# Head-narrow cross attentions tiled in row and column quarters, a wide one in row halves, and other unread products

## What is computed

```python
def _L0_xattn_ref(x, context, mask, g_norm, null_kv, Wq, Wkv, Wout, g_out):
    HEADS, DIM_HEAD = (16, 64)
    ...
    k = jnp.concatenate([nk, k], axis=2)
    v = jnp.concatenate([nv, v], axis=2)
    ...
    sim = jnp.einsum('bhid,bhjd->bhij', q, k)
    ...
    attn = jax.nn.softmax(sim.astype(jnp.float32), axis=-1).astype(sim.dtype)
    out = jnp.einsum('bhij,bhjd->bhid', attn, v)
    ...
def _L2_xattn_ref(query, key_value, Wq, bq, Wk, bk, Wv, bv, Wo, bo):
    ...
    attn = jnp.einsum('bhqd,bhkd->bhqk', q, k) * scale
    attn = jnp.clip(attn, -CLAMP, CLAMP)
    attn = jax.nn.softmax(attn, axis=-1)
    ...
    x = jnp.einsum('bhqk,bhkd->bqhd', attn, v).reshape(B, Nq, Cq)
    return x @ Wo + bo
```

## Time and profile before

| | |
|---|---|
| time, median of 3 runs | 1818.76 us (1816.85 to 1821.48) |
| the profiled execution: its time | 1830.47 us |
| its span | 1828.6 us |
| its mean granted clock of PE | 0.907 |
| PE busy (products) | 1582.6 us, 87% |
| PE weight loads (PEld), beside them | 953.6 us, 52% |
| DVE busy | 1039.3 us, 57% |
| ACT busy | 678.5 us, 37% |
| POOL busy | 376.1 us, 21% |

### The profile page before, as it was taken

One profiled execution on the slowest core, in us unless ns is written; L12 is line 12 of the kernel. 1 busy time (PEld: TensorE's weight loads), 2 busy tenths in 40 slices (PEclk: granted clock), 3 DMA queues, 4 the chain that ended last, 5 costly groups with the idle time before them and its releaser, 6 DMA issues. The chain is left out here.

```text
span 1828.6 us, 24507 instructions
## 1 busy us (share of the span) xinstructions
PE 1582.6 (87%) x9019; PEld 953.6 (52%) x9027; DVE 1039.3 (57%) x1963; ACT 678.5 (37%) x1652; POOL 376.1 (21%) x366
## 2 busy tenths in 40 slices
PE   6999899999999989968988848836989988899996
PEld 3665446445555565554567535522435555564444
DVE  4676574334554555567392366489875554465665
ACT  3774331333555534423102134213555555460001
POOL 3000120001000000033011034255764433410000
PEclk8999999998787889989687979977999999899999
DMA  3000002210000000000104000000111100100000
GB/s 128 2 2 4 1 1 102 97 46 13 1 1 1 1 14 8 9 3 0 60 1 156 9 29 39 20 15 24 35 35 18 18 13 14 17 7 24 23 23 12
DMA packets 14075, 46.92 MB, mean 26 GB/s; under 512 B 3032, under 2 KB 4870, under 8 KB 13328
## 3 DMA queue, kind: packets, MB, share of 16 engines
q1 hardware_dynamic: 13968, 45.49, 8.1%
HBM read 40.73 MB, written 0.56 MB: 23 GB/s over the span
## 5 line engine op out<-in xcount | busy, mean ns | idle before, releaser
L503 DVE TENSOR_REDUCE quad_max<-psum 128x1 f32<-128x128 f32 (+3 forms) x256 | 113.6, 486 | 116.2 <-PE psum L399 115.9
L184 POOL TENSOR_TENSOR rstd<-var,minus_half 128x4 f32<-128x4 f32 x30 | 30.6, 1022 | 655.2 <-DVE var L143 585.5
L468 ACT ACTIVATE pt<-psum,quad_max 128x128 f32<-128x128 f32 (+3 forms) x256 | 133.5, 525 | 83.0 <-DVE quad_max L503 80.5
L193 PE MATMUL psum<-ident 128*128 128x128 f32 x960 | 124.4, 293 | 45.0 <-DVE wide L2069 20.9
L2433 PE MATMUL psum<-slots,xn_t 128*128 128x512 f32 x256 | 113.8, 606 | 42.1 <-DVE pt L2606 42.1
L193 PEld LDWEIGHTS psum<-ident 128*128 128x128 f32 x960 | 120.6, 208 | 49.3 <-DVE wide L2069 21.5
L2469 PE MATMUL psum<-pt,slots 128*128 128x512 f32 x256 | 129.8, 594 | 2.1 <-DVE pt L2619 1.9
L2619 DVE TENSOR_TENSOR pt<-psum,wide 128x512 f32<-128x512 f32 x128 | 87.8, 691 | 52.9 <-PE psum L2462 43.8
L2303 DVE TENSOR_REDUCE duo_max<-psum 128x1 f32<-128x512 f32 x128 | 82.3, 686 | 56.4 <-PE psum L2204 55.3
L415 PE MATMUL psum<-ident,pt 128*128 128x128 f32 x640 | 99.9, 306 | 12.0 <-DVE wide L1212 10.8
L2433 PEld LDWEIGHTS psum<-slots,xn_t 128*128 128x128 f32 x256 | 48.1, 193 | 107.6 <-DVE pt L2606 52.6
(11 more groups left out here) (451 smaller groups left out, 3181.1 us busy)
## 6 DMA issues: line engine op xcount, KB each, us to landing
slots<-in_s_l2f SPq DMA_DIRECT2D x8, 578.0 KB, 3.8
keys_own<-in_s_l2f SPq DMA_DIRECT2D x8, 578.0 KB, 5.6
slots<-in_s_l0f SPq DMA_DIRECT2D x8, 514.0 KB, 3.6
wide<-scratch_gates SPq DMA_DIRECT2D x8, 512.0 KB, 7.6
slots<-in_s_l3v SPq DMA_DIRECT2D x8, 512.0 KB, 3.7
slots<-in_s_l3o SPq DMA_DIRECT2D x8, 512.0 KB, 3.6
weights<-in_w_l1a SPq DMA_DIRECT2D x1, 2624.0 KB, 9.1
weights<-in_w_l0x SPq DMA_DIRECT2D x1, 2113.0 KB, 10.7
```

What stands on the lines that cost most here:

```text
L193: nc.tensor.matmul(m.ps[bank][:, 0:P], m.ident[:, :], m.ident[:, :], start=True, stop=True, skip_group_check=True)
L468: nc.scalar.activation(m.quad_p[:, i % 2, g, 0:keys], m.ps[g][:, 0:keys], ACT.Exp, bias=m.quad_max[:, i % 2, g:g + 1], accum_out=sum_colum ...
L503: nc.vector.tensor_reduce(m.quad_max[:, n % 2, g:g + 1], m.ps[g][:, 0:keys], AX.X, ALU.max, negate=True).then_inc(m.quad_negmax, 1)
```

## The change

The narrow crosses get a loop of their own on PE. Steps go (b, qt, half). Keys are kept in four variants, by which of the four heads in a 32-row quarter a row belongs to (`rows4`), so a score product uses 32 rows, one quarter, and the two products of a step use different quarters and banks. Values are kept in four variants of 32 columns; 16 products (32 output channels, 128 columns) follow once for every two steps, as soon as the second step's copy is done. PE issues 16 and 4 unread products behind the second and third scores. ACT's wait before it overwrites `xpt` follows the new order.

In l0x a score bank gets its mask product first and then four products of 78 columns on 64 rows, the banks alternating; the keys need no zeros. ACT takes over the value copies in the loop and before it, and copies a pair's keys in one instruction; DVE's norm comes ahead of its other work. 14 and 4 unread products stand behind the second and third scores.

`busy_through_norm` gets a third burst behind the first reciprocal root, 4 products unless given; the other bursts change in size (the norms not shown go from 12, 7 or 12, 8 to 12, 6). `turned` issues 4 unread products ahead of its waits. l1x gets 8 unread products in its second iteration. The constants `rows8` and `cols8` are gone.

```diff
@@ -193,10 +193,13 @@
         nc.tensor.matmul(m.ps[bank][:, 0:P], m.ident[:, :], m.ident[:, :], start=True, stop=True, skip_group_check=True)
-def busy_through_norm(nc, pe, m, norm, first, second):
+def busy_through_norm(nc, pe, m, norm, first, second, third=4):
     keep_busy(nc, m, first)
     pe.wait_ge(m.var_ready, 2 * norm)
     keep_busy(nc, m, second)
+    pe.wait_ge(m.rstd_ready, 2 * norm - 1)
+    keep_busy(nc, m, third)
...
-def turned(m, pe, name):
+def turned(nc, m, pe, name):
+    keep_busy(nc, m, 4)
     for j in range(2):
         copied(m, pe, f"{name}{j}")
...
-    busy_through_norm(nc, pe, m, 1, 12, 7)
+    busy_through_norm(nc, pe, m, 1, 12, 6)
...
@@ -674,9 +678,9 @@
         if k < XSTEPS:
             b, half, qt = units[k]
             wait(pe, m.negmax_ready, a.s0 + k - 1)
-            for j in range(2):
-                last = a.scores(m.ps[2 * (k % 2) + j], b, half, j, qt)
-            last.then_inc(m.scores_ready, 1)
+            a.scores([m.ps[2 * (k % 2) + e] for e in range(2)], b, half, qt).then_inc(m.scores_ready, 1)
+            if k in (1, 2):
+                keep_busy(nc, m, (14, 4)[k - 1], 7)
...
+def cross_scalar(nc, act, m, a, units=cross_units()):
+    nk = a.nk
...
-            if b > 0 and qt == 0:
-                a.unit_done(act, b - 1, half)
+            if b > 0:
+                a.unit_done(act, b - 1, half, qt)
...
+        if k in a.scalar_after:
+            a.scalar_after[k](k - min(a.scalar_after))
...
-    busy_through_norm(nc, pe, m, 2, 10, 8)
+    busy_through_norm(nc, pe, m, 2, 8, 8)
...
-    def scores(bank, b, half, j, qt):
-        for i in range(2):
-            g = 4 * half + 2 * j + i
-            nc.tensor.matmul(bank[:, 2 * i * nk:2 * (i + 1) * nk], m.wide[:, g, b * S + qt * P:b * S + (qt + 1) * P],
-                             m.keys_own[:, b, 2 * g * nk:2 * (g + 1) * nk], start=i == 0, stop=False,
+    def scores(banks, b, half, qt):
+        for e in range(2):
+            nc.tensor.matmul(banks[e][:, 0:4 * nk], m.ones_bf[0:1, :], m.mask_row[0:1, b, :], start=True, stop=False,
                              skip_group_check=True)
-        return nc.tensor.matmul(bank[:, 0:4 * nk], m.ones_bf[0:1, :], m.mask_row[0:1, b, :], start=False, stop=True,
-                                skip_group_check=True)
+        for i in range(4):
+            g = 4 * half + i
+            for e in range(2):
+                rows = slice(64 * e, 64 * e + 64)
+                last = nc.tensor.matmul(banks[e][:, i * nk:(i + 1) * nk], m.wide[rows, g, b * S + qt * P:b * S + (qt + 1) * P],
+                                        m.keys_own[rows, b, g * nk:(g + 1) * nk], start=False, stop=i == 3,
+                                        skip_group_check=True)
+        return last
...
-                                    m.xpt[0:nk, half, 2 * i + e, :], start=True, stop=True)
+                                    m.xpt[0:nk, half, 4 * e + i, :], start=True, stop=True)
...
     for g in range(NPAIR):
         bank = read(m, act, f"l0xk{g}")
-        for e in range(2):
-            at = (2 * g + e) * nk
-            last = nc.scalar.activation(m.keys_own[64 * e:64 * e + 64, :, at:at + SC],
-                                        bank[64 * e:64 * e + 64, 0:B * SC].rearrange("p (b k) -> p b k", k=SC), ACT.Copy)
-        last.then_inc(emptied(m, f"l0xk{g}"), 1)
+        nc.scalar.activation(m.keys_own[:, :, g * nk:g * nk + SC], bank[:, 0:B * SC].rearrange("p (b k) -> p b k", k=SC),
+                             ACT.Copy).then_inc(emptied(m, f"l0xk{g}"), 1)
+    for n in range(2 * B):
+        b, j = divmod(n, 2)
+        bank = read(m, act, f"l0xv{n}")
+        nc.scalar.activation(m.context_v[0:SC, b, j * S:(j + 1) * S], bank[0:SC, :], ACT.Copy).then_inc(emptied(m, f"l0xv{n}"), 1)
...
+    def take_values(n):
+        b, half, i = cross_units()[n]
+        bank = read(m, act, f"l0xo{n}")
+        nc.scalar.activation(m.wide[:, 4 * half + i, b * S:(b + 1) * S], bank[:, :], ACT.Copy).then_inc(emptied(m, f"l0xo{n}"), 1)
+    first = NQ + 3
+    a.scalar_after = {first + n: take_values for n in range(XSTEPS + 2 - first)}
     cross_scalar(nc, act, m, a)
+    for n in range(XSTEPS + 2 - first, XSTEPS):
+        take_values(n)
...
+    norm_to_turn(nc, dve, m, twice=True)
...
-    for n in range(2 * B):
-        b, j = divmod(n, 2)
-        bank = read(m, dve, f"l0xv{n}")
-        nc.vector.tensor_copy(m.context_v[0:SC, b, j * S:(j + 1) * S],
-                              bank[0:SC, :]).then_inc(emptied(m, f"l0xv{n}"), 1)
-    norm_to_turn(nc, dve, m, twice=True)
...
-    a.vector_after = {first + n: lambda dve, n=n: take_values(n) for n in range(XSTEPS - first + 1)}
     cross_vector(nc, dve, m, a)
-    for n in range(XSTEPS - first + 1, XSTEPS):
-        take_values(n)
...
-    busy_through_norm(nc, pe, m, 3, 13, 16)
-    busy_through_norm(nc, pe, m, 4, 12, 8)
+    busy_through_norm(nc, pe, m, 3, 12, 6, 12)
+    busy_through_norm(nc, pe, m, 4, 14, 6)
...
+            if k == 1:
+                keep_busy(nc, m, 8, 6)
...
+def narrow_units():
+    return [(b, half, qt) for b in range(B) for qt in range(NQ) for half in range(2)]
...
-        busy_through_norm(nc, pe, m, 10 if clip else 13, 8, 20)
+        busy_through_norm(nc, pe, m, 10 if clip else 13, 10, 6)
...
-        def scores(bank, b, half, j, qt):
-            at = (8 * half + 4 * j) * SC
-            return nc.tensor.matmul(bank[:, 0:4 * SC], m.q_t[:, b * S + qt * P:b * S + (qt + 1) * P],
-                                    m.keys_own[:, b, at:at + 4 * SC], start=True, stop=True)
-        def values(pe, b, half, i):
-            if i == 0:
-                pe.wait_ge(m.narrow_values, a.v0 // 2 + 1)
-            bank = fill(m, pe, f"{stage}o{b}") if half == 0 and i == 0 else m.ps[6 + b]
-            for h in (2 * i, 2 * i + 1):
-                last = nc.tensor.matmul(bank, m.values_own[0:SC, b, 8 * half + h, :], m.xpt[0:SC, half, h, :],
-                                        start=half == 0 and h == 0, stop=half == 1 and h == 7, skip_group_check=True)
-            if i == 3:
-                last.then_inc(filled(m, f"{stage}o{b}") if half else m.pv_done, 1)
-        a.scores, a.values = scores, values
-        cross_tensor(nc, pe, m, a)
+        units = narrow_units()
+        own = lambda g: slice(32 * g, 32 * g + 32)
+        for k in range(XSTEPS + 4):
+            if k < XSTEPS:
+                b, half, qt = units[k]
+                wait(pe, m.negmax_ready, a.s0 + k - 1)
+                for x in range(2):
+                    rows = own(2 * half + x)
+                    last = nc.tensor.matmul(m.ps[2 * (k % 2) + x][:, 0:GROUP * SC], m.q_t[rows, b * S + qt * P:b * S + (qt + 1) * P],
+                                            m.keys_own[rows, b, 0:GROUP * SC], start=True, stop=True)
+                last.then_inc(m.scores_ready, 1)
+                if k in (1, 2):
+                    keep_busy(nc, m, (16, 4)[k - 1], 7)
+            n = k - 2
+            if 0 <= n < XSTEPS:
+                pe.wait_ge(m.probs_ready, a.s0 + n + 1)
+                wait(pe, m.cross_taken, a.x0 + n)
+                for h in range(8):
+                    last = nc.tensor.transpose(m.ps[4 + h // 4][0:SC, (h % 4) * P:(h % 4 + 1) * P],
+                                               m.xp[:, n % 3, h * SC:(h + 1) * SC], m.ident[:, :])
+                last.then_inc(m.turned_ready, 1)
+            n = k - 4
+            if n >= 0 and n % 2 == 1:
+                b, _, qt = units[n]
+                pe.wait_ge(m.cross_taken, a.x0 + n + 1)
+                if n == 1:
+                    pe.wait_ge(m.narrow_values, a.v0 // 2 + 1)
+                bank = fill(m, pe, f"{stage}o{b}") if qt == 0 else m.ps[6 + b]
+                for j in range(GROUP):
+                    for g in range(GROUP):
+                        last = nc.tensor.matmul(bank[own(g), qt * P:(qt + 1) * P], m.values_own[0:SC, b, g, j, :],
+                                                m.xpt[0:SC, g // 2, g % 2 * GROUP + j, qt * P:(qt + 1) * P],
+                                                start=qt == 0 and j == 0, stop=qt == NQ - 1 and j == GROUP - 1,
+                                                skip_group_check=True)
+                last.then_inc(m.pv_done if qt < NQ - 1 else filled(m, f"{stage}o{b}"), 1)
...
-        def unit_done(act, b, half):
-            if half:
+        def unit_done(act, b, half, qt):
+            if qt == NQ - 1:
                 read(m, act, f"{stage}o{b}")
             else:
-                act.wait_ge(m.pv_done, m.pv0 + a.v0 + b + 1)
+                act.wait_ge(m.pv_done, m.pv0 + (NQ - 1) * (a.v0 + b) + qt + 1)
         a.unit_done = unit_done
-        cross_scalar(nc, act, m, a)
+        cross_scalar(nc, act, m, a, narrow_units())
...
-            shape = [P, H, SC]
+            shape = [P, GROUP, SC]
             last = nc.vector.tensor_tensor(
-                m.keys_own[:, b, 0:H * SC].rearrange("p (h k) -> p h k", k=SC),
```

(34 more changed lines are left out.)

44 lines of the change are left out of this document (19 added, 25 removed).

## The result

The kernel after takes 1803.45 us (median of 17 executions, 1790.10 to 1820.41), the kernel before 1822.46 us (17 executions); the ratio is 0.9892, with a 95% interval of 0.9869 to 0.9915. By the ratio that is 19.7 us less (15 to 24); forecast were 15 less than a median of 1818.8, 1804 us.

The account below looks back on a forecast made before the run. A chain over two steps bounds l2x and l3x, PE bounds l0x. Start -3.0, l0x -3.0, l2x -1.9 -12.0, l3x -1.9 -1.3 +1.5, bursts +5.5, l1x +1: -15 from 1818.8 gives 1804 us, range 1775 to 1818.

Parts of the forecast that it names:

- Start, -3.0: Kernel start: engines wait until 14.23 us for constants; dropping cols8 (1088 KB) saves 3.0 us, bounds -1 and -3.5.
- Before the narrow loops, -1.9 each: Ahead of l2x and l3x: DVE's key product falls from 2.78 to 0.7 us, so transposes come 1.9 us earlier.
- Half clock in the narrow loops: l2x and l3x: clock falls to 1.2 GHz behind the bursts until stage end; l2x -12.0 us, l3x -1.3.
- the prediction's own signs of being wrong: Narrow loops at 1.00, l0x at 0.50 beyond step four, an l0x score block over 2 us, first product still at 14.
- The term of -1.3: l3x at half clock: lead 16.4 (-0.6), ten steps of 4.5 us (+5.9), tail 13.0 (-6.6).
- the +1.5 for the output product behind it: Behind l3x: the output product runs at half clock and costs 1.5 us more.
- The full-clock rival: The clock holds in the narrow loops: l2x -28.4, l3x -18.5, about -52 in all, 1767 us; chance 0.25.
- Row and column quarters: l2x, l3x, priced from the quads at full clock: scores 0.79 us against 1.20, values 1.08 against 1.88.
- the upper bound: l0x score block: 3.3 us if each of 16 passes lasts as long as now, plus masks; now 1.92, taken 1.5.
- l0x, -3: l0x: -0.2 us a step over ten steps, -2, and -1 in all from norm, unread products and key copies.
- Bursts, +6.5 with l1x: Unread products: resized norm bursts cost +5.5 us, l1x's +1; those behind the transposes nothing at full clock.
- the opening sentence: Seven tenths of the span get only a few more filler products, so everything large must come from l0x, l2x, l3x.

Follow-up runs that it names:

- narrow_filled: The kernel after, with two unread products in each step of the narrow loops ahead of the wait for the scaled probabilities: 1778.9 us, ratio 0.9788 to the kernel before.
- narrow_alone: The kernel before with only the changed l2x and l3x loops and the two constants gone; l0x and norm bursts essentially as before: 1806.5 us, ratio 0.9927.
- wide_alone: The kernel before with only the changed l0x (row halves, masks first, copies on ScalarE, unread products in the loop): 1812.9 us, ratio 0.9955.
- filled_old_norms: The kernel of narrow_filled with all norm bursts, `turned` and l1x as in the kernel before: 1784.2 us, ratio 0.9773 to the kernel before.

## Why the prediction came out right, step by step

- **Start, -3.0:** 3.1. The first norm gave 1.5 of it back, where the prediction had 0.7.
- **Before the narrow loops, -1.9 each:** from the first context product to the norm's transposes 7.1 us instead of 9.1 in both stages.
- **Half clock in the narrow loops:** right in l2x to the end: lead 18.0, ten steps of 4.90, tail 13.9 us for 18.9, 4.92 and 13.5; in sum -12.8 for -12.0. narrow_filled shows that this level is what the loops pay with: with full clock in most of them the kernel is 19 us faster. In l3x the step that failed is "to stay there to the stage's end": the clock came back, or never fell, and windows at 1.00 were one of the prediction's own signs of being wrong. The term of -1.3 should have been -7.1 by the first profile, -14.2 by the second, and the +1.5 for the output product behind it nothing (2.02 us, at full clock). The full-clock rival gave this stage -18.5, and narrow_alone's profile has it.
- **Row and column quarters:** 0.79 and 1.08 us at full clock, 1.40 and 1.94 at half, as taken from the quads. The drain between tiling modes that the Trainium skill ("TensorEngine Tiling (Array Packing)", Key Properties) states adds nothing that can be seen: value sets and scores follow each other at 1114.47 - 1113.46 = 1.01 us. In l0x, where it would have pushed the block to the upper bound, the block takes 1.41 us; taken were 1.5.
- **l0x, -3:** in after's profile -1.3 before the loop and +0.2 in it, so 2 us short; alone, in twelve executions, -8 (-3 to -14). The step of 3.75 us was right (3.8). Another of those signs came true here: the clock was at 0.50 at the end of the loop, at a cost of 2 us against wide_alone.
- **Bursts, +6.5 with l1x:** +15 alone; as work right by the fit (+7). What was missed is that they move the clock in stages behind them: by the fit +8 for all, +15 for the norms' alone. And the products behind the transposes, costed at nothing, are worth 18 us to the kernel before. So the opening sentence, that everything large must come from three stages since the others get only a few filler products, doesn't hold; those others are some eight tenths of the span, not seven.
- **The sum** of -15 against a measured -19.7 is right in its mechanism and in part lucky in its number: l3x and its output product gave 7 us more than forecast by the first profile, and the bursts cost 8 us more when alone. That 1803.45 us fell beside 1804 is luck too, for the median of the kernel before came out 3.7 us above the 1818.8 that the forecast started from. The parts alone give -15.6, -9.4 and +14.7, in sum -10, and together -18 to -20; the difference is hardly beyond noise, but it goes the way that filled_old_norms shows, where the bursts cost nothing.
- **The rival "the clock holds"** (1767 us) was a mechanism worth making: with two products a step the kernel takes 1779 us, with the old norm bursts 1775.
- **Left open:** what in the narrow loops lets the clock fall. No run fills the gaps with products of 32 rows, so whether the unread products help by their full shape or by their time isn't known.

## What to carry over

Small tiles that are cheap at full clock can cost the clock, as the score quarters did here in part; price both levels, and if the loop leaves gaps, fill them with a little unread work in every step, where the engine waits anyway. One profile is one draw of the clock: compare means of time and of granted clock over ten executions or more before a stage's few us are put down to an edit. Parts that all touch the clock must be tried together, since what they give alone need not be what they give together.

## What the runs showed beside it

- The spread of this kernel's times goes with its mean clock: correlations of -0.94 and -0.97 (before and after), 13 to 14 us per 0.01 of mean granted clock.
- The same narrow loop ran a stage at 1.00 (l3x in narrow_alone, a turn of 6.80 us) and one at 0.50 (l2x in after, 9.98 us), and l3x's loop took 62.2 and 69.3 us in two executions of one program.
- 52 unread products in gaps, in an otherwise unchanged kernel, were worth 1.0% (0.9865 to 0.9933), and longer unread bursts ahead of the transposes lost 1.0% (1.0059 to 1.0142).
